# Causal mask of the scores: from a mask matmul on TensorE to an affine select on GpSimd

## What is computed

```python
qkv = x @ W_qkv + b_qkv                       # x: 1 x 2048 x 512
scores = einsum('bhqd,bhkd->bhqk', q, k) / sqrt(32)
scores = where(tril, scores, -10000)          # causal: a query sees no later key
probs = softmax(scores)
ctx = einsum('bhqk,bhkd->bhqd', probs, v)
return ctx @ W_out + b_out
```

## Time and profile before

| | us |
|---|---|
| median of 3 runs | 2159.66 |
| lowest, highest | 2156.12, 2161.9 |
| the profiled execution | 2161.04 |
| its span in the profile | 2159.3 |
| TensorE busy in the span | 2000.4 (93%) |
| VectorE busy | 1098.8 (51%) |
| ScalarE busy | 638.9 (30%) |
| GpSimd busy | 436.7 (20%) |

### The profile page before, as it was taken

One profiled execution on the slowest core, in us unless ns is written; L12 is line 12 of the kernel. 1 busy time (PEld: TensorE's weight loads), 2 busy tenths in 40 slices (PEclk: granted clock), 3 DMA queues, 4 the chain that ended last, 5 costly groups with the idle time before them and its releaser, 6 DMA issues. The chain is left out here.

```text
span 2159.3 us, 25676 instructions
## 1 busy us (share of the span) xinstructions
PE 2000.4 (93%) x10088; PEld 1415.3 (66%) x10088; DVE 1098.8 (51%) x1908; ACT 638.9 (30%) x1152; POOL 436.7 (20%) x385
## 2 busy tenths in 40 slices
PE   6997799999999999769999999997999869999998
PEld 4675444445444543557888888886887548888886
DVE  4452586677676760664434344334543674344334
ACT  3221144545545556231111111112321232111111
POOL 1124245756564345400000000000000300000000
PEclk9998599999999999979999999999999989999999
DMA  8625331151231100310000000002000002010002
GB/s 306 214 98 149 77 71 39 28 121 42 50 79 32 32 2 1 127 64 30 30 30 30 1 30 30 1 1 79 12 6 10 20 0 79 20 30 10 15 1 78
DMA packets 61720, 111.86 MB, mean 52 GB/s; under 512 B 6000, under 2 KB 21248, under 8 KB 61568
## 3 DMA queue, kind: packets, MB, share of 16 engines
q1 hardware_dynamic: 54144, 85.05, 14.0%
q0 software_dynamic: 7456, 25.18, 3.9%
HBM read 84.77 MB, written 25.44 MB: 51 GB/s over the span
## 5 line engine op out<-in xcount | busy, mean ns | idle before, releaser
L858 DVE TENSOR_REDUCE part_max<-banks 128x1 f32<-128x512 f32 (+2 forms) x640 | 356.4, 613 | 179.9 <-PE banks L734 109.0
L838 ACT ACTIVATE probs<-banks 128x512 f32<-128x512 f32 (+3 forms) x640 | 310.8, 538 | 362.0 <-PE banks L765 194.5
L734 PE MATMUL banks<-kst,qst 96*128 96x512 f32 (+2 forms) x640 | 276.0, 450 | 35.7 <-DVE part_max L858 20.2
L761 PE MATMUL banks<-qst,kst 98*128 98x512 f32 (+2 forms) x640 | 263.7, 423 | 13.9 <-DMA qst<-max_dram 12.3
L1312 DVE TENSOR_TENSOR tokens_a<-banks,tokens_a 128x512 f32<-128x512 f32 x224 | 151.6, 688 | 72.0 <-PE banks L216 70.3
L734 PEld LDWEIGHTS banks<-kst,qst 96*128 96x128 f32 x640 | 132.9, 210 | 82.3 <-DVE part_max L858 57.9
L761 PEld LDWEIGHTS banks<-qst,kst 98*128 98x128 f32 x640 | 125.8, 197 | 86.3 <-issue 54.1
L214 PE MATMUL banks<-h_hi,f_wg_hi 128*128 128x512 f32 x432 | 170.4, 395 | 12.1 <-DVE f_wg_lo L1276 12.1
L1337 DVE TENSOR_TENSOR tokens_b<-banks,tokens_b 128x512 f32<-128x512 f32 x64 | 44.3, 692 | 267.3 <-ACT tokens_b L1258 267.3
L214 PE MATMUL banks<-f_d_hi,f_hid_hi 128*128 128x512 f32 x432 | 171.1, 396 | 5.9 <-issue 3.6
L215 PE MATMUL banks<-h_lo,f_wg_hi 128*128 128x512 f32 x432 | 169.9, 393 | 0.0
(11 more groups left out here) (189 smaller groups left out, 3271.0 us busy)
## 6 DMA issues: line engine op xcount, KB each, us to landing
tokens_a<-in_L_wmod SPq DMA_DIRECT2D x12, 1024.0 KB, 6.9
qst<-q_hi SPq DMA_DIRECT2D x32, 256.0 KB, 5.9
kst<-k_hi SPq DMA_DIRECT2D x32, 256.0 KB, 8.4
tokens_b<-in_L_attn_x SPq DMA_DIRECT2D x4, 1024.0 KB, 13.2
q_hi<-qk_out_hi POOLq DMA_DIRECT2D x16, 256.0 KB, 3.4
q_lo<-qk_out_lo POOLq DMA_DIRECT2D x16, 256.0 KB, 3.4
k_hi<-qk_out_hi POOLq DMA_DIRECT2D x16, 256.0 KB, 3.1
k_lo<-qk_out_lo POOLq DMA_DIRECT2D x16, 256.0 KB, 3.4
```

The lines of the kernel that those rows point to most:

```text
L734: mm = nc.tensor.matmul(dst[:, 0:wide], qst[0:BIASROW, n % QS, h, P * t:P * t + P], kst[0:BIASROW, (NB * g + c) % KS, h, 0:wide], start=Tr ...
L761: mm = nc.tensor.matmul(dst[:, c0:512], kst[0:BIASROW + 2, ck % KS, h, at:at + P], qst[0:BIASROW + 2, n % QS, h, c0:512], start=True, stop ...
L838: nc.scalar.activation(probs[:, q % PS, h, c0:512], bank[3 + sh % 3][:, c0:512], ACT.Exp, scale=SCALE).then_inc(exp_done, 1)
L858: nc.vector.tensor_reduce(part_max[:, n % 2, ht, c:c + 1], bank[slot % 3][:, 0:wide], AX_X, ALU.max).then_inc(max_read, 1)
```

## The change

The mask matmul behind the diagonal scores and its operand `mask_keys` go. The scores of later keys are left as they are, ScalarE exponentiates them, and GpSimd then sets the results of later keys to zero with an affine select, in place: `mask(s)` issues four in each diagonal step, two for each half, each over two heads and the 128 columns that hold the diagonal. The context matmuls of a diagonal step wait for the selects (`masked`) and no longer for the exponentials. The butterflies are split: rounds 0 and 1 come after the selects of the block's first diagonal step, rounds 2 and 3 and the store after those of its second. The max tiles keep their mask matmul.

```diff
-                    nc.vector.tensor_copy(mask_keys[:], stage[:, 2 * P:4 * P])
...
+            def masks_before(s):
+                return 4 * sum(not off_diagonal(q) for q in range(s))
...
+                    def mask(s):
+                        n, i = steps[s]
+                        for half in range(2):
+                            q, c0 = 2 * s + half, P * (2 * i + half - TB * (n % NB))
+                            for pair in range(2):
+                                pool.wait_ge(exp_done, 4 * q + 2 * pair + 2)
+                                here = probs[:, q % PS, 2 * pair:2 * pair + 2, c0:c0 + P]
+                                nc.gpsimd.affine_select(out=here, in_=here, pattern=[[0, 2], [1, P]],
+                                                        compare_op=ALU.is_ge, fill=0.0, base=0,
+                                                        channel_multiplier=-1).then_inc(masked, 1)
+
-                    def butterflies(s):
+                    def butterflies(s, rounds):
                         cols = slice(FW * s, FW * s + FW)
                         pool.wait_ge(fw_loaded, 16 * (s + 1))
-                        for r in range(4):
+                        for r in rounds:
...
-                        pool.dma_start(w2m[:, :, cols], fw[0]).then_inc(fw_stored, 16)
+                        if r == 3:
+                            pool.dma_start(w2m[:, :, cols], fw[0]).then_inc(fw_stored, 16)
...
                         if off_diagonal(s):
                             add_pair(s)
-                        elif i == 2 * (n % NB) and n in mixed_at:
-                            butterflies(mixed_at[n])
+                            continue
+                        mask(s)
+                        if n in mixed_at:
+                            butterflies(mixed_at[n], (0, 1) if i == 2 * (n % NB) else (2, 3))
...
-                        mm = nc.tensor.matmul(dst[:, c0:512], kst[0:BIASROW + 2, ck % KS, h, at:at + P],
-                                              qst[0:BIASROW + 2, n % QS, h, c0:512], start=True, stop=(t < 0))
-                        if t >= 0:
-                            mw = 2 * P if t == 3 else P
-                            mm = nc.tensor.matmul(dst[:, c0:c0 + mw], ident16[:], mask_keys[:, 2 * P - mw:2 * P],
-                                                  start=False, stop=True)
-                        mm.then_inc(score_mm, 1)
+                        nc.tensor.matmul(dst[:, c0:512], kst[0:BIASROW + 2, ck % KS, h, at:at + P],
+                                         qst[0:BIASROW + 2, n % QS, h, c0:512], start=True,
+                                         stop=True).then_inc(score_mm, 1)
...
-                            pe.wait_ge(exp_done, 4 * q + 4)
+                            if diagonal:
+                                pe.wait_ge(masked, masks_before(s) + 2 * half + 2)
+                            else:
+                                pe.wait_ge(exp_done, 4 * q + 4)
```

More of the change, by code:

```diff
@@ L69, in build_program @@
         ident16 = sb(whole, "ident16", [P, P], BF16)
-        mask_keys = sb(whole, "mask_keys", [P, 2 * P], BF16)
         mask_queries = sb(whole, "mask_queries", [P, 2 * P], BF16)
@@ L565, in build_program @@
             ones_ready = sem(ctx, "ones_ready")
+            masked = sem(ctx, "masked")
             max_mm = sem(ctx, "max_mm")
@@ L754, in score @@
                             pe.wait_ge(ones_ready, KS + 1)
-                        t = kt - TB * j
                         c0 = min(first_column(n, kt), 2 * P)
```

## The result

The changed kernel takes 2179.82 us (median of 4 runs, 2172.28 to 2179.91), the kernel before 2160.78 beside it (2156.12 to 2163.59). The ratio is 1.0081, with a 95% interval of 1.0060 to 1.0102: slower by 0.8%. Forecast were 2157.3 us, and 2142 to 2172 for eight in ten.

What follows compares the result with a forecast made beforehand. TensorE was taken to set the pace on average, VectorE or ScalarE in single stretches. -8.3 - 1.0 + 0.8 + 1.2 + 5.0 + 0 = -2.3 us gave 2157.3 as the runs' median, 2142 to 2172 for eight in ten.

Steps and rivals of the forecast that it cites:

- -8.3 - 1.0 + 0.8: Attention: masks gone where TensorE paces, first score sooner where ScalarE paces, block 15's last tile waiting for its select, in us.
- VectorE's chain: Maxima chain waiting for GpSimd: one hit goes (-4), two chains beside a delayed add_pair (+4); taken 0, bounds -5 and +12.
- The store and the pairs: Rounds 2 and 3 behind selects delay store, load and add_pair: block 5 +3.5 us, block 9 +1.5; bounds 0 and 12.
- Late columns of blocks 4 and 8: Load behind the previous block's masks makes butterflies and selects late for the context matmuls by 0.6 us each: +1.2.
- Block 2's relief: VectorE's chain hit at 358.27 goes, with TensorE's 2.31 us stop and half clock behind it: about -4 us.
- The masks: Removing 256 mask matmuls in the attention gains 9.3 us, bounds 1 and 16.
- The sorting by pace: Masks by pacing engine: VectorE 84, gaining nothing; ScalarE 40, gaining 1 us in all; TensorE 132, gaining 8.3.
- The select: 128 GpSimd selects between exponentials and context matmuls: 0.69 us each, bounds 0.31 and 1.3.
- Rival 2: Slow select, from 1.1 us on, makes TensorE wait in most tails; about 2176 us at 1.3; chance 0.13.
- Rival 4: GpSimd pays for some 50 switches between select and add; 2166 us at 1 us each; chance 0.04.
- Rival 3: Selects and late adds block VectorE's chain, three more hits: +12, so 2169 us; chance 0.09.
- Rival 1: Whole gain arrives, VectorE-paced stretches shrink too: -8 to -17, so 2143 to 2152 us; chance 0.18.

Runs made afterwards that it cites:

- e5: Changed kernel with the cast, copy and subtraction of VectorE's chain written as reductions; 2154.36 us, ratio 0.9967.
- e8: Changed kernel with only the loads of blocks 1, 2, 5, 6 and 9 moved behind the first add_pair; 2153.26 us, ratio 0.9965.
- e6: Changed kernel with both the loads moved behind add_pair and VectorE's chain written as reductions; 2128.56 us, ratio 0.9849.
- e7: Kernel before with VectorE's chain written as reductions, nothing else; 2143.64 us, ratio 0.9920.
- e4: Changed kernel with the butterflies' loads moved behind an add_pair, for blocks 4 and 8 the last one of the block ahead; 2150.61 us, ratio 0.9946.
- e3: Kernel before without the scores' mask matmul and without selects, so the probs' causal mask is left out; 2147.61 us, ratio 0.9939.
- e10: Changed kernel with only the cast and copy of VectorE's chain as reductions, the subtraction left as it was; 2164.77 us, ratio 1.0023.
- e9: Kernel before with the butterflies' loads moved behind an add_pair, nothing else; 2161.16 us, ratio 0.9999.
- e1: Kernel before with only the butterflies split over the two diagonal steps, mask matmul kept, no selects; 2163.48 us, ratio 1.0012.

## Why the prediction was wrong

The runs split the +19.2 us (2179.8 - 2160.6, the kernel before beside e5 to e8) into three, by differences between kernels that were timed, each known to some 5 us:

| | measured | how | the prediction's term |
|---|---|---|---|
| the mask matmul goes, selects come, queue and chain in order | -15.1 | e6 - e7 | -8.3 - 1.0 + 0.8 |
| loads, store and pairs late | +25.8 | e5 - e6 | +5.0 + 1.2 |
| VectorE's chain held up more | +8.5 | 25.5 (after - e5) less 16.9 (before - e7) | 0 |
| sum | +19.2 | | -2.3 |

The split depends on the order: with the chain left as it was, the late queue is worth 29.2 (after - e4), since a pile of adds is also what holds the chain. With the loads moved the cast is back at 612 ns, so that what the chain lost by the change hangs on the late queue as well.

1. **The store and the pairs: the step that failed.** It is the term +5.0 (with the columns +6.2, bounded by 12), and 25.8 was measured. The mechanism was right, down to the buffer: block 5's exponentials wait for `add_pair` behind a load behind a landing. Its size was not. Forecast: store at 448.9, landing 5 to 8.5 us, `add_pair` at 455.5, +3.5 us in block 5 and +1.5 in block 9, 12 at the most. Measured: store at 449.77, load 10.1 us behind it, `add_pair` at 461.06, and the total with the columns 25.8. Two things were missed. 455.5 is the time for a landing of 5.4 us; the landing seen right there, 8.5, would have given 458.5. Block 5 then lost 7 us from its start to block 6's, against 3.5, and block 9 3.6 to its third step, against 1.5. And "the others lose less than they have" took each block by itself: the delay of one block's `add_pair` passes to the next store, so block 6 was hit again: its load stood 5.59 us, and the adds behind it held the cast of point 2, in all +8.8 us in one step.
2. **VectorE's chain, taken as 0 with hits that last one GpSimd instruction.** Block 2's relief came as forecast: -3.6 against -4 (after minus before falls from +4.3 at its step 3 to +0.7 at step 4). But a hit isn't bounded by one instruction. In block 6 the cast lasted through a row of seven adds, 8.65 us, and at 282.72 another through three, 3.50 us; both rows stood right behind a load that had waited for its store (5.59 and 4.87 us), as in point 1. The count of hits was near (19 before, 17 after), the size of one far off. The bound of +12 held the measured +8.5; the value of 0 did not. Nor did I see that the chain's hits were 16.9 us of the kernel before: the means of its three lines, 559, 621 and 448 ns where an undisturbed one takes some 170, come to 18 us over the 16 blocks.
3. **Late columns of blocks 4 and 8**: +1.2 forecast, between 3 and 10 measured (e8 against e4), for another reason than the select's length. The load issued at 429.33 (forecast 430) let the butterflies start only 8.2 us later, not 5.5.
4. **The masks**: -9.3 forecast, -13.75 measured alone (e3). The sorting by pace held where it was read at full clock: little where VectorE paces, 0.1 to 0.2 us a step in block 5. A mask where TensorE paces is worth 1.56/16 = 0.10 us in the mean rather than 0.0625, in the end of block 7, and 1.54/16 again between e7 and e6; which widths are worth more wasn't read. Over 132 masks that would be 13 instead of 8.3, an estimate. Block 0 at half clock gave 3.4 against a forecast of 0. That TensorE's busy time would fall by 60 us was wrong as well: over the whole span it is 2000.4 us before, 1985.3 in e3 and 1992.2 in the changed kernel, since time in which matmuls overlap is counted once.
5. **The select**: taken 0.69, measured 0.406, inside its bounds, and below 0.69 the sum hardly asks. Rival 2 falls. By the memset's row, to which the rule of the Trainium skill's GPSIMD Engine Reference (section 4.1, Engine selection) led, it would be 0.31; the measured one lies nearer to that than to the add's. By the prediction's own reading this was worth 2 us at most, and TensorE's waits for selects are 2.5 in all. Rival 4 falls: no configuration change stands at the switches.
6. **Rival 3** named the right place (late adds on VectorE's chain) and a price of 12, against 8.5. It was a part of what happened, but not by more hits, by two long ones, and these went when the loads were moved (e4); the prediction had treated them as alternatives. Rival 1's gain is real in size (-15.1 of its -8 to -17), but reached only by a kernel with the queue in order, and not for its reason: from e7 to e6 block 5's steps shrink by only 0.1 to 0.2 us, and blocks 0 to 2 give 6.5. The Trainium skill's Advanced Engine Details and Errata (VectorE Performance Modes, Mode Summary) says that GpSimd's instructions and VectorE's two-port ones block each other over a shared port. Both traces agree for the cast and the copy, with 170 ns undisturbed against 8.65 us; the summary gives no size. That the subtraction with two SBUF operands is held too is what e10 shows.

What stays open: why one cast is held by a single add and another by seven. In both long cases of the changed kernel (8.65 and 3.50 us) the adds came right behind a load that had waited, and in e4, with those waits gone, no cast took over 1.23 us; no run parts that from chance of arrival. It isn't that the adds stand back to back: in the kernel before a cast came into a row as dense, four adds from 384.80 to 389.80 without a gap, and was held by one of them:

```profile
387.38 1.22 DVE L871 CAST neg_hi<-neg_max 128x16 fp32r<-128x16 f32 x1
388.63 1.20 DVE L873 COPY neg_parts<-neg_hi 128x16 f32<-128x16 f32 x1
```

Nor was it tried whether the longer landing of the store, up to 10.1 us, comes from SyncE's loads that run beside it.

## What to carry to other kernels

When work is put into an in-order queue, list what is queued behind it that waits for something, here a store's landing, and follow the delay through the next rounds, not one; a wait placed ahead of other work costs nothing while nothing urgent stands behind it (26.9 us of such waits before, e9) and can cost all it has once something does, and moving it behind that work (e4) turned +19 us into -11. Short VectorE copies beside long GpSimd adds are to be read by their spread, not their median: the same values written as reductions gave 17 us in the kernel before, and with the loads moved as well the change is worth another 15 (e6, the best version: 2128.56, 32 below before). The worth of a matmul in a pipeline is the distance of starts with it and without it, at the clock of that very stretch.

## What the runs showed of the hardware

- An affine select on GpSimd of 2 x 128 fp32 elements a partition took 406 ns (396 to 419), where an add of 512 takes about 1.23 to 1.28 us and a memset of 256 would take 0.31 by the earlier trace rows.
- A VectorE cast of 16 elements a partition took 0.17 us alone and up to 8.65 us beside a row of GpSimd adds; the same cast written as a reduction took 0.169 to 0.171 us every time, and the copy's replacement 0.157 to 0.161 in e5 and 0.170 to 0.171 in e10. The subtraction with two SBUF operands is held too (620 ns mean, up to 1.91 us in e10).
- In eight traces 131 of these short VectorE instructions took over 0.35 us. Each ended 0.02 to 0.05 us behind the end of a GpSimd instruction, 122 times an add, nine times a select.
- From GpSimd's issue of a store to the next load that waits for its landing took 8.5 us before, 8.0 in e1, 10.1 after, 9.7 in e4 and 10.5 in e5, for the same transfer. The load took 5.7 us to the first butterfly in the earlier trace rows (with GpSimd free all the while) and 8.2 in the changed kernel.
